# Cross-attention in one decoder layer: head outputs projected undivided, the reciprocal sums applied at the residual

## The reference, cut to what matters

```
q = (x @ w_q).reshape(b, n, 16, 64)
k, v = (context @ w_kv) split and shaped the same way
attn = softmax(einsum('bnhd,bmhd->bhnm', q, k) * 64**-0.5)
out = einsum('bhnm,bmhd->bnhd', attn, v).reshape(b, n, 1024)
x = layernorm(x + out @ w_out + b_out)
```

## Time and profile before

| | |
|---|---|
| median of three runs | 2048.67 us (2048.62 to 2049.02) |
| the profiled execution's own time | 2053.94 us |
| its span, first to last instruction | 2052.2 us |
| mean granted TensorE clock | 0.919 |
| PE busy | 1746.8 us (85%) |
| DVE busy | 1191.0 us (58%) |
| POOL busy | 1323.0 us (64%) |
| ACT busy | 832.0 us (41%) |

### The profile page before, as it was taken

The page is one execution under the profiler, slowest core; times in us unless marked ns, Lnnn a source line. Parts: engine busy times, 40 slices in busy tenths (PEclk is TensorE's granted clock), DMA queues, the critical chain, the costliest instruction groups (busy, mean ns, idle before and its releaser), DMA issues. The chain is left out here.

```text
span 2052.2 us, 32755 instructions
## 1 busy us (share of the span) xinstructions
PE 1746.8 (85%) x10682; PEld 1212.3 (59%) x10682; DVE 1191.0 (58%) x2046; ACT 832.0 (41%) x1228; POOL 1323.0 (64%) x711
## 2 busy tenths in 40 slices
PE   7553599999989999998999999899999998509990
PEld 5443466666656666665666666566666664408980
DVE  4788555556565656556565665655565654553345
ACT  3111234444444444444444444444444444224440
POOL 2988338577676667576776676675766677454544
PEclk8775689999999999999999999999999999559995
DMA  5000200000200000010000001000000000321223
GB/s 185 1 21 24 79 1 22 1 22 0 73 1 22 22 3 22 0 52 22 21 1 23 1 21 52 21 22 1 21 1 21 15 1 1 124 84 63 71 63 128
DMA packets 37813, 68.09 MB, mean 33 GB/s; under 512 B 3560, under 2 KB 27504, under 8 KB 36656
## 3 DMA queue, kind: packets, MB, share of 16 engines
q1 hardware_dynamic: 33936, 56.12, 8.1%
q0 software_dynamic: 3744, 10.23, 1.5%
HBM read 52.84 MB, written 13.50 MB: 32 GB/s over the span
## 5 line engine op out<-in xcount | busy, mean ns | idle before, releaser
L1001 POOL TENSOR_TENSOR xa_total<-xa_total,xa_pexp 128x1024 f32<-128x1024 f32 (+1 forms) x352 | 852.9, 2423 | 52.7 <-ACT xa_pexp L942 27.3
L1060 DVE TENSOR_REDUCE xa_parts<-ps_ring 128x1 f32<-128x402 f32 x1024 | 532.3, 565 | 299.8 <-PE ps_ring L887 292.8
L942 ACT ACTIVATE xa_pexp<-ps_s 128x1024 f32<-128x1024 f32 (+1 forms) x416 | 422.7, 1025 | 419.0 <-PE ps_s L842 391.9
L856 PE MATMUL ps_pv<-xa_pexp,xa_v 128*64 128x512 f32 (+1 forms) x1664 | 399.8, 604 | 0.0
L887 PE MATMUL ps_ring<-xa_k_hi,xa_q_hi 64*128 64x402 f32 x1024 | 235.0, 377 | 32.7 <-DVE xa_parts L1060 31.4
L856 PEld LDWEIGHTS ps_pv<-xa_pexp,xa_v 128*64 128x64 f32 (+1 forms) x1664 | 106.2, 137 | 181.9 <-issue 148.3
L887 PEld LDWEIGHTS ps_ring<-xa_k_hi,xa_q_hi 64*128 64x128 f32 x1024 | 142.7, 186 | 118.2 <-DVE xa_parts L1060 58.9
L1001 POOL TENSOR_TENSOR xa_total<-xa_pexp 128x1024 f32<-128x1024 f32 x32 | 76.3, 2384 | 190.9 <-ACT xa_pexp L942 189.6
L1048 DVE TENSOR_TENSOR xa_k_lo<-ps_ring,xa_k_hi 128x402 fp32r<-128x402 f32 (+1 forms) x128 | 73.6, 575 | 214.7 <-ACT xa_k_hi L953 214.7
L842 PE MATMUL ps_s<-xa_q_hi,xa_k_hi 64*128 64x512 f32 (+1 forms) x832 | 194.0, 433 | 3.6 <-DVE xa_k_lo L1048 2.8
L842 PE MATMUL ps_s<-xa_q_neg,xa_row_one 64*128 64x512 f32 (+1 forms) x832 | 174.4, 393 | 0.0
(11 more groups left out here) (263 smaller groups left out, 2946.2 us busy)
## 6 DMA issues: line engine op xcount, KB each, us to landing
wa_raw<-in_pack_a SPq DMA_DIRECT2D x17, 768.0 KB, 4.4
ex_w_raw<-in_pack_e SPq DMA_DIRECT2D x8, 1026.0 KB, 5.3
ctx_raw<-in_ctxT SPq DMA_DIRECT2D x4, 1601.0 KB, 8.5
wb_raw<-in_pack_b SPq DMA_DIRECT2D x16, 256.0 KB, 2.6
ex_w_hi<-ybuf SPq DMA_DIRECT2D x8, 512.0 KB, 7.6
sa_xT<-in_xT SPq DMA_DIRECT2D x8, 256.0 KB, 6.4
X<-in_x SPq DMA_DIRECT2D x1, 2048.0 KB, 11.5
x_hi<-sa_x1s_hi SPq DMA_DIRECT2D x16, 128.0 KB, 2.1
```

The source lines that it names most:

```text
L856: ins = nc.tensor.matmul(ps_pv[half(h), :], v[0:m, t, at:at + XD], pexp[0:m, buf, h, :], start=t == 0, stop=t == MT - 1)
L942: nc.scalar.activation(pexp[0:m, buf], ps_s[0:m, (p * MT + t) % 2], ACT.Exp, scale=XD ** -0.5)\
L1001: nc.gpsimd.tensor_tensor(total[p][0:m], first, pexp[0:m, buf], ALU.add).then_inc(s["add_done"], 1)
L1060: nc.vector.tensor_reduce(parts[:, h, q, c:c + 1], ps_ring[:, r, 0:CW], AX.X, ALU.max)\
```

## The change

The sums `ps_pv` are no longer divided ahead of the projection. ACT copies them as `att_hi` where it copied `pv_sb`, and DVE makes `att_lo` from `ps_pv` at t = 0 of the next block (R4). PE forms the row sums the other way round: `total[p]`, 128 queries at a time, is the stationary operand and one column of ones the moving one, eight matmuls in all, so that the sums stand as [128 queries, 2 heads x 4]; DVE takes their reciprocal straight from the bank. R1, R2, R3 and ACT's copy of the sums are gone. The projection is done for each head by itself: 64 rows by 256 columns, head 0 into one bank and head 1 into the next, so that OP j takes two banks. OP 0 stands at t = 4 and OP 1 at t = 6, each behind that t's MX pair. DVE adds with eight instructions per block (2 j x 2 heads x 2 halves of a bank), each of them 128x256 times a reciprocal per partition plus the residual.

```diff
--- before.py
+++ after.py
@@ -576,9 +576,12 @@
 
 def chain(p, back):
 
-    return {3: ([("RS", p)], []), 4: ([], [("R1", p, 0)]), 5: ([], [("R1", p, 1)]), 6: ([], [("R1", p, 2)]),
-            7: ([], [("R1", p, 3), ("R2", p)]), 8: ([], [("R3", p), ("R4", p)]),
-            9: ([], [("OP", p, 0, back), ("OP", p, 1, back)])}
+
+    return {0: ([], [("R4", p)]), 3: ([("RS", p)], []), 4: ([], project_out(p, 0, back)), 6: ([], project_out(p, 1, back))}
+
+
+def project_out(p, j, back):
+    return [("OP", p, j, h, back) for h in range(2)]
 
 
 def join(*parts):
@@ -598,8 +601,7 @@
     tail = [("SH", 1)] + ([] if last else first_keys(0))
     steps = block(0, join(own, loads, {} if first else chain(1, 1)), maxima_of(1), tail)
     if last:
-        end = [("RS", 1)] + [("R1", 1, k) for k in range(4)] + [("R2", 1), ("R3", 1), ("R4", 1),
-                                                               ("OP", 1, 0, 0), ("OP", 1, 1, 0)]
+        end = [("R4", 1), ("RS", 1)] + project_out(1, 0, 0) + project_out(1, 1, 0)
         return steps + block(1, chain(0, 0), [], end)
     nxt = {1: ([], [("K", 0, 2), ("K", 0, 3)]), 6: ([], [("WB",)])}
     values = {t: ([], [("V", t - 3), ("V", t - 2)]) for t in range(3, MT, 2)}
@@ -735,17 +737,17 @@
         total = [sb(f"total{p}", [P, 2, N]) for p in range(2)]
         parts = sb("parts", [P, 2, NC, 4])
         negmax = sb("negmax", [P, NC, P])
-        pv_sb, sums, inv, att = (sb(x, [P, N]) for x in ("pv_sb", "sums", "inv", "att"))
+        row_raw, inv = sb("row_raw", [P, P]), sb("inv", [P, 2, 2, NC])
         att_hi, att_lo = sb("att_hi", [P, N], F32R), sb("att_lo", [P, N], F32R)
 
         ps_s = ctx.enter_context(nc.psum_tensor("ps_s", [P, 2, 2, N], F32))
         ps_pv = ctx.enter_context(nc.psum_tensor("ps_pv", [P, N], F32))
         ps_ring = ctx.enter_context(nc.psum_tensor("ps_ring", [P, RING, 512], F32))
 
-        s = sems(ctx, nc, "ones_set zero_set scores_ready exp_done pv_done add_done pv_copied att_ready "
+        s = sems(ctx, nc, "ones_set zero_set scores_ready exp_done pv_done add_done att_ready "
                           "k_hi_done q_hi_done shift_ready x1_in ctx_hi_done ctx_lo_done "
-                          "wa_hi_done wa_lo_done wb_hi_done wb_lo_done att_done att_hi_done filled0 filled1 filled2 "
-                          "drained0 drained1 drained2 inv_ready")
+                          "wa_hi_done wa_lo_done wb_hi_done wb_lo_done att_hi_done filled0 filled1 filled2 "
+                          "drained0 drained1 drained2")
         s.update(loads.sems)
         filled = [s[f"filled{r}"] for r in range(RING)]
         drained = [s[f"drained{r}"] for r in range(RING)]
@@ -845,7 +847,7 @@
                 elif kind == "PV":
                     p, t = st[1:]
                     if t == 0:
-                        need(pe, s["pv_copied"], n.of("COPY"))
+                        need(pe, s["att_ready"], n.of("COPY"))
                         if p == 0:
                             r, c = n.job(("V", MT - 1))
                             pe.wait_ge(drained[r], c)
@@ -907,19 +909,26 @@
                     r = take_bank(n)
                     pe.wait_ge(s["add_done"], n.of("ADD"))
                     for h in range(2):
-                        ins = nc.tensor.matmul(ps_ring[half(h), r, :], ones[:, 0:XD], total[p][:, h, :],
-                                               start=True, stop=True)
+                        for q in range(NC):
+                            at = h * NC + q
+                            ins = nc.tensor.matmul(ps_ring[:, r, at:at + 1], total[p][:, h, q * P:(q + 1) * P], ones[:, 0:1],
+                                                   start=True, stop=True)
                     ins.then_inc(filled[r], 1)
                 elif kind == "OP":
-                    p, j = st[1:3]
+                    p, j, h, back = st[1:]
                     r = take_bank(n)
-                    pe.wait_ge(s["att_ready"], n.of("R4"))
+                    if h == 0:
+                        pe.wait_ge(s["att_ready"], n.of("R4"))
+                        return
+                    banks = (n.job(("OP", p, j, 0, back))[0], r)
                     for q in range(2):
                         cs = slice((2 * j + q) * P, (2 * j + q + 1) * P)
-                        terms = [(att_hi[:, cs], w_out(wa_hi, p)), (att_lo[:, cs], w_out(wa_hi, p)),
-                                 (att_hi[:, cs], w_out(wa_lo, p))]
-                        ins = project(ps_ring[:, r, q * E:(q + 1) * E], terms)
-                    ins.then_inc(filled[r], 1)
+                        for k, (x, w) in enumerate(((att_hi, wa_hi), (att_lo, wa_hi), (att_hi, wa_lo))):
+                            for g in range(2):
+                                ins = nc.tensor.matmul(ps_ring[:, banks[g], q * E:(q + 1) * E], x[half(g), cs], w_out(w, p)[half(g)],
+                                                       start=k == 0, stop=k == 2)
+                                if q == 1 and k == 2:
+                                    ins.then_inc(filled[banks[g]], 1)
 
             def t_of(n):
                 return n.here.get("S", 0) % 2
@@ -943,8 +952,7 @@
                         .then_inc(s["exp_done"], 1)
                 elif kind == "PV" and st[2] == MT - 1:
                     act.wait_ge(s["pv_done"], n.of("PV") + 1)
-                    need(act, s["att_done"], n.of("R2"))
-                    nc.scalar.copy(pv_sb[:], ps_pv[:]).then_inc(s["pv_copied"], 1)
+                    nc.scalar.copy(att_hi[:], ps_pv[:]).then_inc(s["att_hi_done"], 1)
                 elif kind == "K":
                     p, c = st[1:]
                     r = n.slot()
@@ -957,14 +965,6 @@
                     r = n.slot()
                     act.wait_ge(filled[r], n.of("ring%d" % r) + 1)
                     nc.scalar.copy(q_hi[p][:], ps_ring[:, r, :]).then_inc(s["q_hi_done"], 1)
-                elif kind == "RS":
-                    r = n.slot()
-                    act.wait_ge(filled[r], n.of("ring%d" % r) + 1)
-                    need(act, s["inv_ready"], n.of("R1"))
-                    nc.scalar.copy(sums[:], ps_ring[:, r, :]).then_inc(drained[r], 1)
-                elif kind == "R3":
-                    act.wait_ge(s["att_done"], n.of("R3") + 1)
-                    nc.scalar.copy(att_hi[:], att[:]).then_inc(s["att_hi_done"], 1)
                 elif kind == "SH":
                     p = st[1]
                     r = n.slot()
@@ -1025,12 +1025,12 @@
         @block.vector
         def _(dve):
             nc.vector.memset(negmax[:], 0.0)
-            nc.vector.memset(att[:], 0.0).then_inc(s["zero_set"], 1)
+            nc.vector.memset(row_raw[:], 0.0).then_inc(s["zero_set"], 1)
             dve.wait_ge(s["zero_set"], 1)
             for h in range(2):
-                nc.vector.memset(att[h * XD:h * XD + 1, 0:P], 1.0).then_inc(s["zero_set"], 1)
+                nc.vector.memset(row_raw[h * XD:h * XD + 1], 1.0).then_inc(s["zero_set"], 1)
             dve.wait_ge(s["zero_set"], 3)
-            nc.vector.tensor_copy(row_one[:], att[:, 0:P]).then_inc(s["ones_set"], 1)
+            nc.vector.tensor_copy(row_one[:], row_raw[:]).then_inc(s["ones_set"], 1)
 
             def handle(i, n, st):
                 kind = st[0]
@@ -1066,28 +1066,26 @@
                     for h, col in ((0, 0), (1, XD)):
                         nc.vector.tensor_reduce(negmax[:, :, col:col + 1], parts[:, h], AX.X, ALU.max, negate=True)\
                             .then_inc(s["shift_ready"], 1)
-                elif kind == "R1":
-                    if st[2] == 0:
-                        r, c = n.job(("RS", st[1]))
-                        dve.wait_ge(drained[r], c)
-                        need(dve, s["att_done"], n.of("R2"))
-                    cs = slice(st[2] * N // 4, (st[2] + 1) * N // 4)
-                    nc.vector.reciprocal(inv[:, cs], sums[:, cs]).then_inc(s["inv_ready"], 1)
-                elif kind == "R2":
-                    dve.wait_ge(s["inv_ready"], n.of("R1"))
-                    dve.wait_ge(s["pv_copied"], n.of("R2") + 1)
-                    need(dve, s["att_ready"], n.of("R4"))
-                    nc.vector.tensor_tensor(att[:], pv_sb[:], inv[:], ALU.mult).then_inc(s["att_done"], 1)
+                elif kind == "RS":
+                    r = n.slot()
+                    dve.wait_ge(filled[r], n.of("ring%d" % r) + 1)
+                    nc.vector.reciprocal(inv[:, st[1]].rearrange("p h q -> p (h q)"), ps_ring[:, r, 0:2 * NC]).then_inc(drained[r], 1)
                 elif kind == "R4":
                     dve.wait_ge(s["att_hi_done"], n.of("R4") + 1)
-                    nc.vector.tensor_tensor(att_lo[:], att[:], att_hi[:].bitcast(F32), ALU.subtract)\
+                    nc.vector.tensor_tensor(att_lo[:], ps_pv[:], att_hi[:].bitcast(F32), ALU.subtract)\
                         .then_inc(s["att_ready"], 1)
                 elif kind == "OP":
-                    p, j, back = st[1:]
```

(11 more changed lines are left out.)

## The result

The changed kernel takes 2153.79 us (median of four runs, 2150.87 to 2155.67), the kernel before 2048.85 beside it: a ratio of 1.0507, 95% interval 1.0489 to 1.0525. It is slower, as forecast, but by 105 us instead of 56, and it lies above the stated range (2072 to 2142).

A forecast was written before the change was run, and what follows sets the result against it. PE's order was taken to set the time in the rounds. Block terms +12.8, -4.5 and +31.7, row sums +19.5 and the end -3.1 made +56 us on 2053.94: 2110, about 2105 for the runs, range 2072 to 2142.

The forecast's parts named there:

- part 3: OP needs two banks, which DVE holds longer: waits of 3.47 us per block, net loss 1.07 (block 0) or 1.98 (block 1).
- The walk: Stepping through one block's PE order with each bank's return time: five waits, sum 3.47 us, bounds 2.6 and 5.2.
- the fourth wait: The extra MX pair ahead of S(7) waits 1.14 us for a bank held by head 0's adds.
- part 2: OP as 24 matmuls of 64 rows with overlapping halves: 0.75 us per OP, 1.50 against 1.61, counted as no change.
- the rival without overlap: OP's 64-row halves do not overlap: +1.2 us per block, 2142 us; chance 0.08.
- part 4: Row sums by one-column matmuls: 1.44 us instead of 0.91, plus a mode change of 0.10, so +0.63 per block.
- part 5: At three batch ends PE's lost time falls from 7.47 to 3.9 us; with the other waits -1.5 each.
- part 6: End of the last block, from RS to the last addition, at half clock: gain 3.1 us.
- The first rival: Faster: DVE's shed work decides and OP's bank waits are covered; 2020 us for the runs, chance 0.08.
- part 1: Removing the reciprocals ends PE's waits behind DVE: 1.66 us in block 0 and 0.75 in block 1.
- No change: Rival: both sides cancel, with RS at 0.91 and the walk 1.3 us per block too long; 2049 us, chance 0.04.

## Why the prediction was right and where it was wrong

**Ring of banks (part 3), right.** The walk's five waits of 0.82, 0.20, 0.86, 1.14 and 0.45 were 0.92, 0.28, 0.93, 1.03 and 0.43. Blocks without a half-clock stretch lengthen, from RS to RS, from 41.0 to 42.9 us (block 0) and from 50.1 to 53.0 (block 1). Less 0.96 for RS that is 0.94 and 1.94, against 1.07 and 1.98 (of blocks 1 without a stretch there is only one). Moving OP behind PV took most of it back. Some of the closeness is luck. By the walk's own times the fourth wait is 10.15 less 9.19 (OP 1's end at 9.1 and 0.09 for the first MX) = 0.96, not 1.14; an add of 128x256 took 0.480 (84.3 us for 192), not 0.42, which puts the bank back 0.1 later. The two slips partly cancel: 1.06 from the walk, 1.03 measured.

**OP's matmuls (part 2), right.** 0.78 for six pairs with 0.75 forecast; the rival without overlap falls: such an OP would have taken 1.4.

**Row sums (part 4), the first term that was mis-sized.** RS is 1.87, not 1.54 with its mode change: a record costs 0.117, nearly the 0.114 of the shift's records that I had kept as the upper end; 1, 64 or, in the shift, 128 columns cost nearly the same. 31 x 0.33 = +10 us. The error was in reading the gate, more than in halving it. Its 0.72 us divided by four gives 0.18, but in the trace only its first record is short, 0.073 to the second; from there the starts are 0.213 apart, the next matmul's included: a record of a stream cost 0.213 at half clock already there. RS at half clock in the last block shows the same 0.213 from start to start, and at full clock 0.112, so halving is nearly right. The Trainium skill ("TensorE: Matmul & The Clock Gate", section "LDWEIGHTS (loading the stationary operand)") had 0.107 for each load, an estimate of 1.71 us that came nearer than my choice; the measurement is a tenth above it. The page's formula names no clock, and at half clock it does not hold here: the last RS, at 1.2 GHz, takes 0.217 per record:

```profile
1851.12 3.54 PE L914 MATMUL ps_ring<-ones,xa_total 128*128 128x1 f32 x16 [4.00 <-POOL xa_total L1001]
1854.59 0.58 PE L928 MATMUL ps_ring<-xa_wa_hi,xa_att_hi 64*128 64x256 f32 x2
```

**The clock, the step that was missing.** Part 3 counted each wait at its length and part 4 the loads at theirs; the prediction assumed that the granted clock of 1.00 in the rounds would stay. The one loss of clock before, at a batch's end, stood unnamed in the 7.47 us of part 5; the prediction did not ask whether the two waits around OP 1, or the one-column matmuls of RS, could bring it on inside a block. 9 stretches x 1.7 and 15 x 1.2 (the sixteenth cost nothing, below) = +33 us of the 49 that were missed, against +10 from RS: this is the larger part. Both causes are shown apart: OP behind PV removes one kind, RS in fp32r or with 64 columns the other, and with OP moved and RS in fp32r none is left. The range did not hold such a term; nor did it reach up to the walk's own upper bound of 5.2 us per block (+54), which would have covered the time for a wrong reason.

**Where a batch ends (part 5), direction right.** The hole of 5.94 us became one of 2.96:

```profile
599.53 0.45 PE L889 MATMUL ps_ring<-xa_k_hi,xa_q_hi 64*128 64x402 f32 x1
602.94 0.45 PE L889 MATMUL ps_ring<-xa_k_hi,xa_q_hi 64*128 64x402 f32 x1 [2.96 <-DVE xa_parts L1060]
603.03 0.59 PE L844 MATMUL ps_s<-xa_q_hi,xa_k_hi 64*128 64x512 f32 x2
```

RS to RS the three blocks take 47.4, 47.9 and 48.3 before and 46.8 each after: less 0.96 that is -1.6, -2.0 and -2.4, on average -2.0 for the forecast -1.5. One of the three has a stretch at t = 7 after the change and is no longer than the other two: what it costs is gone again in the wait of 2.96, and it is not counted above. **The end (part 6):** from the last RS to the end of the span 300.5 before and 298.0 after, -2.5 for -3.1.

**The books.** From the first RS to the last 1425.9 us before and 1528.6 after, +102.7. RS 31 x 0.96 = 29.8, banks 12 x 0.94 + 16 x 1.94 = 42.3, batch ends 3 x -2.0 = -6.0, clock 33.3: 99.4. The 3.3 left over stands mostly in two blocks 1 (59.4 and 57.6 us), which are 1.6 and 1.2 longer than these terms make them, and I can't place it. The forecast for the same stretch was +59.5; RS and clock add 44 to that, the batch ends give 1.5 back and the banks 2. Ahead of the first RS the trace is 3.3 shorter, so the two profiled spans differ by 96.9; that the medians differ by 105 comes from the profiled executions, 5 above its median before and 3 below it after.

**The first rival** (DVE's relief decides) falls. What the reciprocals cost was even less than part 1 allowed: with them in place and the MX pair moved, the two distances that it read for them fell from 1.05 to 0.27 and from 1.21 to 0.60. That error of part 1 did not reach the sum, which compares whole waits. With that pair moved in both, the kernel before takes 1999.8 us and the change with OP behind PV and RS in fp32r 2018.0, on the same chip. **No change** falls with RS: it needed 0.91 for RS and waits 1.3 shorter than the walk's, and neither is there.

## What to carry to other kernels

A ring of banks is paid by the time until the slowest reader gives a bank back, so walk the jobs in order with that time; the walk came within about 0.1 us of each of five waits, and it also shows which single job to move. Put a job that needs two banks behind work that needs none. When a matmul is made narrow to reshape its output, price it by its weight loads, and look at the granted clock behind it; and before crediting a faster operation with a wait, take away the crowd in front of it and see whether the wait is still there.

## What the runs showed of the hardware that I had not expected

- Sixteen records with 128-column loads and one moving column take 1.87 us at full clock and 3.47 at half; with 64 moving columns 1.92. As eight fp32r records with two columns they take 0.98.
- Behind the one-column form TensorE fell to 1.2 GHz in 9 to 22 of some 30 blocks, in 28 when it was twice as long, and in none with 64 columns or in fp32r, though PE was shown as busy throughout. A busy PE row is no sign that its clock is safe.
- Two waits of 0.93 and 1.03 us with 0.8 us of matmuls between them brought half clock on in 16 of 31 blocks, at 1.2 us each, more than either wait. With the first at 0.83 and the second gone none came (the change with the MX pair moved), nor with the 0.74 and 0.75 of the kernel before. Why half of the blocks were spared stays open.
